# A low-rank expert stage with experts on partitions, rotary tables moved to it, and norm statistics taken at the ends of two stages

## The reference

```
x = x + tanh(g_xattn[i]) * xattn_i(layernorm(x), ctx, ...)
x = x + tanh(g_ffn[i])   * ffn_i(layernorm(x), ...)
```

## Time and profile before

| | |
|---|---|
| median of three runs | 1014.83 us |
| profiled execution | 1008.54 us, span 1006.8 us |
| PE busy | 887.8 us (88%) |
| DVE busy | 699.0 us (69%) |
| ACT busy | 609.2 us (61%) |
| POOL busy | 400.8 us (40%) |
| mean granted TensorE clock | 0.961 |

### The profile page before, as it was taken

The page is one execution under the profiler, slowest core; times in us unless marked ns, Lnnn a source line. Parts: engine busy times, 40 slices in busy tenths (PEclk is TensorE's granted clock), DMA queues, the critical chain, the costliest instruction groups (busy, mean ns, idle before and its releaser), DMA issues. The chain is left out here.

```text
span 1006.8 us, 17419 instructions
## 1 busy us (share of the span) xinstructions
PE 887.8 (88%) x5622; PEld 554.4 (55%) x5628; DVE 699.0 (69%) x1405; ACT 609.2 (61%) x1196; POOL 400.8 (40%) x339
## 2 busy tenths in 40 slices
PE   9799979998999999995897689998559999957788
PEld 4555546435777777773575543332425666645436
DVE  6999977988666666666787768995542334238876
ACT  5799925886777777775564457888303433205563
POOL 2899400684555454542331370000023677210122
PEclk9899999999999999999899799999879999979989
DMA  4332076000000000000000202300493332240001
GB/s 127 130 125 84 2 233 184 12 11 11 19 18 16 21 17 21 16 10 6 2 1 1 58 2 86 106 3 2 152 346 83 53 74 45 35 120 0 1 1 42
DMA packets 44287, 57.29 MB, mean 57 GB/s; under 512 B 5704, under 2 KB 35152, under 8 KB 44224
## 3 DMA queue, kind: packets, MB, share of 16 engines
q1 hardware_dynamic: 37728, 48.33, 14.8%
q0 software_dynamic: 4416, 6.03, 3.6%
q10 hardware_dynamic: 2080, 2.10, 0.6%
HBM read 49.90 MB, written 6.49 MB: 56 GB/s over the span
## 5 line engine op out<-in xcount | busy, mean ns | idle before, releaser
L1415 POOL TENSOR_TENSOR a_scratch<-a_scratch,a_inverse 128x512 f32<-128x512 f32 x64 | 66.6, 1041 | 117.0 <-DVE a_inverse L1551 117.0
L2628 PE MATMUL bank<-wup,moe_xT 128*128 x184 | 83.0, 594 | 1.2 <-ACT moe_xT L2690 1.1
L2412 DVE TENSOR_REDUCE a_tops<-bank 128x4 f32<-128x1024 f32 x64 | 77.7, 1223 | 8.5 <-PE bank L2092 5.5
L2863 DVE TENSOR_TENSOR moe_act_f<-bank,moe_silu 128x512 f32<-128x512 f32 x23 | 15.9, 692 | 93.2 <-ACT moe_silu L2697 81.5
L2260 ACT ACTIVATE wup<-bank,a_exp_scale 128x1024 f32<-128x1024 f32 x64 | 71.2, 1114 | 13.7 <-PE bank L2115 13.7
L1334 ACT ACTIVATE a_scratch<-bank,a_bias,a_q_factor 128x256 f32<-128x256 f32 x128 | 71.1, 560 | 10.0 <-DVE a_bias L1538 9.2
L573 POOL TENSOR_TENSOR ssm_drive<-ssm_du,ssm_b_row 128x1024 f32<-128x1024 f32 x32 | 74.5, 2368 | 3.2 <-DVE ssm_state L648 2.0
L648 DVE TENSOR_TENSOR_SCAN ssm_state<-bank,ssm_drive 128x512 f32<-128x512 f32 x64 | 74.7, 1208 | 0.6 <-POOL ssm_drive L573 0.2
L1146 PE MATMUL bank<-keys,a_scratch 128*128 (+1 forms) x256 | 69.1, 392 | 1.8 <-DVE xn L1478 0.7
L2690 ACT COPY moe_xT<-bank 128x256 f32<-128x256 f32 x23 | 8.6, 372 | 100.4 <-PE bank L2616 100.4
L2755 POOL DMA_INDIRECT moe_x_rows<-moe_y,moe_token x23 | 43.8, 1904 | 58.6 <-DVE moe_y L2870 45.3
(11 more groups left out here) (504 smaller groups left out, 2326.9 us busy)
## 6 DMA issues: line engine op xcount, KB each, us to landing
ssm_b_row<-ssm_b_spill SPq DMA_DIRECT2D x16, 512.0 KB, 3.6
wup<-in_l_up_dram SPq DMA_DIRECT2D x8, 1024.0 KB, 9.5
a_wq_in<-in_l1x_q_dram SPq DMA_DIRECT2D x32, 128.0 KB, 2.1
wdn<-in_l_down_dram SPq DMA_DIRECT2D x8, 512.0 KB, 10.9
keys<-in_l1x_o_dram SPq DMA_DIRECT2D x1, 2048.0 KB, 13.3
X<-in_x_dram SPq DMA_DIRECT2D x1, 1024.0 KB
lora_raw<-in_l_gate_dram SPq DMA_DIRECT2D x1, 1024.0 KB, 4.9
lora_raw<-in_l_up_dram SPq DMA_DIRECT2D x1, 1024.0 KB, 7.1
```

What stands on the lines that cost most here:

```text
L1415: pool.tensor_tensor(prob[:, j, :, :], prob[:, j, :, :], inverse[:, j, :].unsqueeze(2).to_broadcast([P, 2, SEQ]), ALU.mult).then_inc(S["p_ ...
L2412: dve.tensor_reduce(tops[:, f // 2 % 3, :, first:first + 2].rearrange("p q h -> p h q"), bank[:, at:at + 2, :].rearrange("p h (q n) -> p h ...
L2628: last = pe.matmul(bank[:, 2 * (i % 2) + m, :], xT[:, i % 2, c, :], wup[:, bass.ds(e, 1), c * 2 * FF + m * FF:c * 2 * FF + (m + 1) * FF] . ...
```

## The change

1. **Low-rank stage.** `hidden` now has `A`'s expert rows on partitions and 512 tokens along the row (8 groups: 4 blocks of expert rows by 2 halves of tokens), so its product needs no transpose. The unscaled one-hot choice is turned (8 transposes to 8 x 128), copied as bf16, and spread by a constant 8 x 512 bf16 matrix (`spread`) over expert rows; ACT copies that mask to SBUF, DVE multiplies. The softmax weight and gate go into the final add. DVE's ternary work stands in another order.
2. **Tables of `a32` in the low-rank stage.** Weights `turn_q`, `turn_kv` and positions are loaded during `ssm`. The bound of the context is taken in the head of `ssm`, all else between `xn` and the choice, or behind the choice.
3. **`a16` and `bit` look ahead.** Statistics, roots and reciprocals of the next norm come at their ends.
4. **End of `bit`.** The last two `down` go to banks 0 and 1. PE gets 22 matmuls with no use for their result (`keep_busy`).
5. **Head of `a32`.** Three such matmuls ahead, no table work; the first projection waits for the first half of `xnT` alone; POOL's clearing of `slots` waits for `xn`.

```diff
@@ stage_ssm: SP, DVE @@
+                sp.dma_start(core.low_select[:, :].rearrange("p (e r) -> p e r", e=8),
+                             d["select3"][0:8, 0:8 * P].rearrange("p (e r) -> p e r", e=8)[:, :, 0:64]).then_inc(core.low_in, 16)
...
+                sp.dma_start(core.turn_kv[:, :], d["l2x_kv"]).then_inc(core.turn_in, 16)
+                sp.dma_start(core.turn_q[:, :, :], d["l2x_q"].rearrange("(c p) n -> p c n", p=P)).then_inc(core.turn_in, 16)
+                sp.dma_start(core.turn_pos[:, :, :], d["pos"].rearrange("(t p) k -> p t k", p=P)).then_inc(core.turn_in, 16)
...
+                dve.wait_ge(S["in_s"], 2 * 16)
+                dve.tensor_reduce(core.tall[:, 3:4], ctxT[:, :], AX.X, ALU.max, apply_absolute_value=True)
@@ stage_lora_moe: PE @@
-                        last = pe.matmul(bank[:, t % 2, :], core.xnT[:, c, t * P:(t + 1) * P], wA[:, c, :],
+                        last = pe.matmul(bank[:, H_BANK[g], :], wA[:, c, j * P:(j + 1) * P], core.xnT[:, c, h * HALF:(h + 1) * HALF],
                                          start=c == 0, stop=c == DC - 1)
...
+                def spread(g):
+                    j, h = GROUPS[g]
+                    pe.wait_ge(chosen_ready, 2)
+                    await_count(pe, mask_ready, g - 1)
+                    pe.matmul(bank[:, M_BANK[g % 2], :], core.low_select[:, j * P:(j + 1) * P], chosen[:, h * HALF:(h + 1) * HALF],
+                              start=True, stop=True).then_inc(spread_done, 1)
...
+                for g in range(4, 8):
+                    hidden(g)
+                    spread(g - 2)
+                spread(6)
+                out(0)
+                spread(7)
+                out(1)
@@ stage_lora_moe: ACT @@
+                act.preload_act_table_set("trig_and_small")
+                act.wait_ge(angles_ready, 1)
+                act.activation(trig[:, :, :, :], angle[:, :, :, :], ACT.Sin).then_inc(trig_done, 1)
...
+                for g in range(len(GROUPS)):
+                    act.wait_ge(spread_done, g + 1)
+                    await_count(act, masked, g - 1)
+                    act.copy(mask[:, g % 2, :], bank[:, M_BANK[g % 2], :]).then_inc(mask_ready, 1)
@@ stage_lora_moe: DVE @@
+                def choose(g):
+                    j, h = GROUPS[g]
+                    dve.wait_ge(h_done, g + 1)
+                    dve.wait_ge(mask_ready, g + 1)
+                    dve.tensor_tensor(hmT[:, j, h * HALF:(h + 1) * HALF], bank[:, H_BANK[g], :], mask[:, g % 2, :], ALU.mult
+                                      ).then_inc(masked, 1)
@@ stage_attention_16: end of DVE @@
                 mix_low(2 * NH - 1, 0)
+                dve.wait_ge(S["added"], 2)
+                s.ahead_stats_of(dve, range(NT // 2))
                 bring(2 * NH - 1, 1)
+                s.ahead_aggr_of(dve, range(NT // 2))
                 mix_low(2 * NH - 1, 1)
                 for j in range(2):
                     add(1, j)
+                    dve.wait_ge(S["added"], 3 + j)
+                    s.ahead_stats_of(dve, range(4 + 2 * j, 6 + 2 * j))
+                s.ahead_aggr_of(dve, range(NT // 2, NT))
+                for h in range(2):
+                    s.ahead_reciprocal(dve, h)
@@ stage_bitnet: PE @@
                 down(NT - 3)
-                for t in (NT - 2, NT - 1):
-                    turn_fq(t)
-                    down(t)
+                turn_fq(NT - 2)
+                keep_busy(4)
+                down(NT - 2)
+                keep_busy(6)
+                turn_fq(NT - 1)
+                keep_busy(4)
+                down(NT - 1)
+                keep_busy(8)
@@ stage_bitnet: DVE @@
                 for t in range(NT):
                     if t >= 3:
                         add(t - 3)
                     await_count(dve, fq_ready, t)
                     butterflies(t)
+                    if t >= 3:
+                        statistics(t - 3)
+                s.ahead_aggr_of(dve, range(NT // 2))
                 for t in range(NT - 3, NT):
                     add(t)
+                    statistics(t)
+                s.ahead_aggr_of(dve, range(NT // 2, NT))
@@ stage_attention_32: PE, POOL, DVE @@
+                for _ in range(3):
+                    pe.matmul(bank[:, 5, :], core.ident[:, :], wq[:, :, :].rearrange("p c n -> p (c n)"), start=True, stop=True)
                 s.norm_tensor(pe)
-                pe.wait_ge(S["tall_ready"], 1)
...
+                pool.wait_ge(s.xn_ready, NT)
...
+                s.normalise_vector(dve)
                 dve.memset(bank[:, 6:8, 0:SEQ], 0.0).then_inc(S["banks_clear"], 1)
-                s.norm_vector(dve)
-
-                dve.wait_ge(S["w_in"], 5 * 16)
-                dve.tensor_reduce(tall[:, 0:2], wq[:, :, :], AX.X, ALU.max, apply_absolute_value=True)
...
```

More of the change, by code:

```diff
@@ L732, in stage_lora_moe @@
         l_rows = s.sb("l_rows", [P, SEQ])
-        hm = s.sb("hm", [P, 2, ER])
-        hmT = s.sb("hmT", [P, 2, JC, P])
+        hmT = s.sb("hmT", [P, JC, NTOK])
+        chosen = s.sb("chosen", [NE, NTOK], BF16)
+        mask = s.sb("mask", [P, 2, HALF], BF16)
+        weight = s.sb("weight", [P, NT])
         NW = DC * BIT_FF
@@ L811, in _ @@
                 last.then_inc(logits, 1)
-                for t in range(NT):
-                    if t + 1 < NT:
-                        hidden(t + 1)
-                    turn(t)
+                pe.wait_ge(tall_ready, 1)
+                pe.matmul(bank[:, 6, 0:2], core.ones[:, :], bound[:, :], start=True, stop=True).then_inc(bound_done, 1)
+                hidden(1)
+                hidden(2)
+                pe.wait_ge(hot_ready, 1)
+                for t in range(NT):
+                    last = pe.transpose(bank[0:NE, M_BANK[t // 4], t % 4 * P:(t % 4 + 1) * P], hot[:, t, :], core.ident[:, :])
+                last.then_inc(hot_turned, 1)
+                hidden(3)
+                spread(0)
+                spread(1)
+                for g in range(4, 8):
[5 more added lines that the diff above has]
+                out(1)
+                pe.wait_ge(sums, 3)
+                pe.wait_ge(masked, 6)
+                pe.matmul(bank[:, 6, 0:3], core.ones[:, :], rowsum[:, :], start=True, stop=True).then_inc(sums_out, 1)
+                for t in range(2, NT):
                     if t == 5:
                         pe.wait_ge(weighed, 7)
-                        pe.matmul(bank[:, 7, 0:12], core.ones[:, :], sizes[:, :], start=True, stop=True).then_inc(sizes_out, 1)
-                    if t >= 1:
-                        out(t - 1)
-                    if t == 3:
-                        pe.wait_ge(sums, 3)
-                        pe.matmul(bank[:, 7, 0:3], core.ones[:, :], rowsum[:, :], start=True, stop=True).then_inc(sums_out, 1)
-                out(NT - 1)
+                        pe.matmul(bank[:, 5, 0:12], core.ones[:, :], sizes[:, :], start=True, stop=True).then_inc(sizes_out, 1)
+                    out(t)
             @block.scalar
@@ new lines, in _ @@
+                row_sum(0)
+                for g in range(4):
+                    choose(g)
+                row_sum(1)
+                choose(4)
+                choose(5)
+                row_sum(2)
+                choose(6)
+                choose(7)
+                add(0)
+                add(1)
+                dve.wait_ge(sums_out, 1)
+                chain(dve.tensor_scalar(wmean[:, :], bank[:, 6, 0:3], 1.0 / (NW * P), BIT_EPS, ALU.mult, ALU.max))
+                chain(dve.reciprocal(wscale[:, :], wmean[:, :]))
@@ new lines, in _ @@
+                chain(dve.reciprocal(core.wback[:, :], wscale[:, :]))
+                scaled(0)
+                add(2)
+                rounded(0)
+                add(3)
+                bounded(0)
+                scaled(1)
+                add(4)
+                rounded(1)
+                add(5)
+                dve.wait_ge(sizes_out, 1)
+                dve.tensor_reduce(size[:, :], bank[:, 5, 0:12].rearrange("p (k n) -> p k n", k=3), AX.X, ALU.add).then_inc(sized, 1)
+                bounded(1)
@@ L1883, in quantize @@
                             dve.tensor_scalar(uback[:, cols], back[:, cols], wback[:, 1:2], None, ALU.mult).then_inc(xq_scaled, 1)
-                for h, tiles in enumerate(halves):
-                    quantize(h, tiles)
+                quantize(0, halves[0])
+                quantize(1, halves[1])
                 dve.wait_ge(xq_scaled, 2)
@@ L1960, in stage_attention_32 @@
         ident16 = s.sb("ident16", [P, P], F16)
[L1961 to L1965 removed]
+        cos8, sin8, exp_scale = core.cos8, core.sin8, core.exp_scale
         straight, crossed = s.sb("straight", [P, 2, 2 * DM]), s.sb("crossed", [P, 2, 2 * DM])
@@ L2354, in _ @@
-                for c in (TURN_HI, TURN_LO):
-                    chain(dve.scalar_tensor_tensor(angle[:, :, :, :], turns[:, :, :, :], -c, angle[:, :, :, :],
-                                                   ALU.mult, ALU.add))
```

(5 more changed lines are left out.)

258 lines of the change are left out of this document (124 added, 134 removed).

## The result

| | before | after |
|---|---|---|
| median | 1011.83 us (4 executions) | 997.83 us (4) |
| profiled execution | 1008.54 us | 997.88 us |
| its span, mean granted clock | 1006.8 us, 0.961 | 996.2 us, 0.971 |

The ratio is 0.9869, 95% interval 0.9838 to 0.9900: faster by 1.3%, a little more than the 1% that the prediction took as the least that a measurement tells from no change. It had given 0.56 to a result within that 1% and 0.39 to a faster one. The forecast was -8.1 us; the two profiles differ by 10.6 us, the medians by 14.0. The median lies 0.17 us under the lower end of the range. Later series add 63 executions of before (1006.1 to 1015.0 us, median 1010.4) and six of the changed kernel (ten in all: 997.5 to 1002.1, median 998.4). One more execution of before took 1529.8 us at a mean clock of 0.553, a slow state that is left out everywhere.

What follows compares the result with a forecast made beforehand. It took each changed stage to have its own limit, with DVE, not PE, ending the low-rank stage. Terms -0.5 - 0.2 - 3.7 - 3.7 = -8.1 us against the 1014.83 us median gave 1006.7 us, range 998 to 1012.

Steps and rivals of the forecast that it cites:

- the four places: Low-rank stage, end of `a16` with head of `bit`, end of `bit`, head of `a32`: together -8.1 us.
- Low-rank stage: From the choice to `half_scale`: DVE sets the end, 171.5 instead of 172.02, -0.5 us; ends -3.3 and +2.2.
- DVE's list plus its waits: Low-rank stage: 26.0 us of DVE work, 2.2 of it tables, plus 3.0 of waits puts `half_scale` at 171.7.
- PE's step of a group: Low-rank stage: masks 2 and 3 come every 1.71 + 0.22 us, so DVE waits 1.0 and 1.3 us.
- the rival: Low-rank stage: PE was the bound after all; -3.3 us there, sum -10.9, 1003.9 us; chance 0.14.
- End of `a16`: End of `a16` and head of `bit`: first `xn` at 475.2 against 475.27, -0.2 us; ends -0.6 and +1.1.
- End of `bit`: End of `bit`: earlier add and statistics put the first `xn` of `a32` at 555.8 instead of 559.51, -3.7 us.
- Head of `a32`: Head of `a32`: first rotation 6.2 us after first `xn` instead of 9.9, -3.7 us; ends -4.3 and +0.7.
- arrives before 560.5: Head of `a32`: the context, now first in the queue, lands before ACT's first half copy ends at 560.5.
- Clock low at the start of `a32`: Rival, head of `a32`: half speed loses 4.4 us of the gain, sum -3.7, 1011.1 us; chance 0.14.
- Slower, clock low in the low-rank stage: Rival, low-rank stage: PE's clock falls inside it, about +18 us there, sum +10, 1025 us; chance 0.04.
- two pairs of equal right: Four earlier executions of before taken as pairs: 1007.77 and 1008.54, 1014.83 and 1015.1; trace from lower, median from upper.

Runs made afterwards that it cites:

- tables_late: Changed kernel with the table work of `a32` back in the head of `a32`, behind its `xn`; median 1003.78 us, ratio 0.9892 to 0.9950 to before.
- a16_order: Changed kernel with the four early statistics at the end of `a16` behind `bring` instead of ahead of it; median 998.04 us, ratio 0.9856 to 0.9897 to before.
- no_busy: Changed kernel without its 25 matmuls of no use (22 at the end of `bit`, 3 at the head of `a32`); median 1002.75 us.
- ctx_split: Changed kernel without the three f32 matmuls at the head of `a32`, context loaded as two pieces; median 996.37 us, ratio 0.9827 to 0.9889 to before.
- before_again: The kernel before once more, not edited, for a second profile; median 1009.23 us, ratio 0.9960 to 1.0021 to before.
- one_bank: Changed kernel with all eight `down` products in bank 6 again, each waiting for the add before it; median 1003.66 us, ratio 0.9888 to 0.9947 to before.

## Why the prediction was right, and where it was wrong

The mechanism was right: the four places change by 0.1 + 0.3 + 3.8 + 3.4 = 7.6 us, forecast 0.5 + 0.2 + 3.7 + 3.7 = 8.1.

- *Low-rank stage.* Near the forecast by luck, with the working wrong. `half_scale` came 29.18 us behind the choice (29.3 before), and I had 28.8. But the sum "DVE's list plus its waits" treated the 2.2 us of table work as additional; `tables_late` shows 0.2. The mis-sized term is PE's step of a group, 2.23 us and not 1.93: the four f32 instructions take 1.91 before the bf16 product can start, not 1.71, and that product 0.32, not 0.22. In the first 18 us PE sets the pace, as the rival said, and behind that DVE does. The rival's -3.3 supposed a DVE that never waits; it waited 3.4 us for masks.
- *End of `a16`.* -0.28 for -0.2, and `a16_order` confirms the cost of the early statistics: 0.7 net of the 1.1.
- *End of `bit`.* 5.91 us from the last `fq` to the first `xn`; the working gave 6.0. The 0.4 us behind `keep_busy` was there (0.27 back with two fewer). Two edits share the gain, and neither does it alone: 9.17 us without the statistics, 10.56 without the banks.
- *Head of `a32`.* 6.51 for 6.2: a little more at each step. PE began with `xn` and not 0.1 us ahead of it, the three matmuls held it 2.65 us for 2.6, the first turnings took 1.07 for 1.0, and from PE's first product to the rotation it was 1.57 us for 1.5. That the context "arrives before 560.5" was true: it landed at 557.1. What the working left out is that this load varies, and at 5.0 us becomes the bound once the three matmuls go, as in `no_busy`.
- *Clock low at the start of `a32`* (0.14): not so in either profile of the changed kernel (1.00 from 544 to 600). It was so in `no_busy` and not in `ctx_split`, one profile each, which points to the 22 matmuls at the end of `bit`, not the three at the head of `a32`, as what keeps it up. The Trainium skill's remark that short idle times can send the clock back and forth ("TensorE: Matmul & The Clock Gate", section "A second HAM failure mode: psum-queue depth-cycling") fits the first profile of before, 0.54, 0.61, 0.82 and 0.75 in the four stretches from 556 to 572. It fits neither `before_again`, 0.50 in all of them, nor the changed kernel.
- *Slower, clock low in the low-rank stage* (0.04): it didn't fall inside, but in some executions just behind it, which cost 1.7 us. PE is idle longer there than before, 0.73 us busy of 172 to 176 against 1.98; that this is the cause is argued, not shown.

The step that failed is the last one, from the difference to a time. I set -8.1 us against a median of three, 1014.83, and took the executions for two pairs of equal right. In 67 executions before has no two groups but spreads over 9 us, with 1010.4 in the middle, and two of the first three lay at the top. From 1010.4 the sum gives 1002.3, still 3.9 us over the 998.4 of the changed kernel. The whole difference of 12.0 us is 7.6 in the four places, 1.7 in `a16`'s loops, which no step of mine has, and 2.7 for which there is only an argument from two profiles of before: the low clock at the end of `bit` and the head of `a32`, which varies there and was not seen after the change.

## What to carry to other kernels

Read what stands behind a waiting instruction on its engine before pricing the wait: one bank cost 4.65 us, of which the wait made 1.3 beyond the moment the next operand was ready, and the queue behind it 3.2. Two gains that overlap aren't a sum (3.26 us at the first `xn` were 1.46 at the rotation); undo each alone to see which part is paid twice. Where a result is needed by another engine's last work of a stage, make it first: `half_scale` moved 4.5 us up the same list and gave 1.1.

## What the runs showed of the hardware

- A stretch with PE partly busy can stay at 1.2 GHz for 20 us: clock 0.50 from 552 to 572 in `before_again` with PE busy 1.2 to 3.9 of each 4 us, while the same program in its first profile had 0.54 to 1.00 there. An execution of before takes longer the lower its mean clock: 1006 us at 0.964, 1015 at 0.951.
- 3.3 us of an idle PE at a stage's end were followed by full clock in some executions (176 to 180: 1.00 in the changed kernel's two) and by 0.59 and 0.62 in others of the same instructions up to there (`one_bank`, `no_busy`), which cost 1.7 us.
- A bf16 product over 512 columns between f32 groups took 0.32 us of PE's time (150.87 to 151.19), where such products in a row take 0.22.
- The loops of `a16` ran 1.5 to 1.9 us apart in two programs that have the same instructions there, in all three profiles of one and both of the other; where this comes from wasn't found.
- One load of 512 KB landed 3.5 us after its issue in the changed kernel and 5.0 us in `no_busy`; split, its first 64 KB landed after 1.9 us and the rest after 3.3.
